# Row stores issued by SyncE and half of the cap computed by GpSimd in the message pass of a graph network kernel

## The reference, cut to what matters

```python
total = concat([atom_fea[dst], atom_fea[src], edge_fea], axis=1)
total = batchnorm(total @ fc_w.T + fc_b, bn1_w, bn1_b)
gate, core = split(total, 2, axis=1)
messages = sigmoid(gate) * softplus(core)
aggr = segment_sum(messages, dst)
```

## Time and profile before

| | |
|---|---|
| Median of three runs | 10762.31 us (10761.59 to 10765.0) |
| The profiled execution | 10770.62 us, of which the span in the trace is 10768.9 us |
| Message pass, first to last exp (L1103) | 5573.0 to 6329.5 us |
| VectorE, GpSimd, TensorE busy in the span | 62%, 65%, 52% |
| ScalarE busy in the span, and in 5700 to 6300 us | 21%, 81% |

### The profile page before, as it was taken

How to read it: one execution, slowest core, us unless ns; L and a number is a source line. 1 busy time by engine, 2 the same in 40 slices (tenths; PEclk the granted TensorE clock), 3 DMA queues, 4 the chain that set the end, 5 groups by cost and what they waited for, 6 DMA issues and landing times.

```text
span 10768.9 us, 124090 instructions
## 1 busy us (share of the span) xinstructions
PE 5555.5 (52%) x33901; PEld 4489.6 (42%) x33999; DVE 6624.7 (62%) x9196; ACT 2252.0 (21%) x3204; POOL 6998.2 (65%) x7048
## 2 busy tenths in 40 slices
PE   4566666457777566666654433333333433333333
PEld 3444444357777454545432213333333333333333
DVE  6777777888831455555568865555555555555556
ACT  1111111146620011111138841111111111111111
POOL 6777777523411777777765546777777577777774
PEclk8877777678989788888865555666556665555556
DMA  8777777423466677777756634555555345555552
GB/s 180 197 196 194 200 193 197 121 114 153 165 242 270 209 231 240 233 239 234 238 196 203 201 112 104 123 126 124 126 124 125 82 119 124 125 124 126 124 126 69
DMA packets 2332510, 1784.10 MB, mean 166 GB/s; under 512 B 1805237, under 2 KB 1977018, under 8 KB 2322746
## 3 DMA queue, kind: packets, MB, share of 16 engines
q1 hardware_dynamic: 759943, 879.12, 24.9%
q10 hardware_dynamic: 1356944, 617.91, 21.0%
q0 software_dynamic: 215456, 284.72, 11.5%
HBM read 921.34 MB, written 861.11 MB: 166 GB/s over the span
## 4 chain that ended last, share of the span: by engine, by line
POOL 54%; issue 22%; DVE 8%; DMA 6%; PE 4%; ACT 4%; SPq 1%; ACTq 1%; POOLq 0%; DVEq 0%
POOL arena L592 51%; DMA arena<-near_d,dlo 2%; ACT arena L1103 2%; DMA feat<-adj_d 2%; PE ph L914 2%; POOL feat L684 2%; DVE obuf L1881 1%; POOL sum_d L625 1%; ACT obuf L1073 1%; DMA arena<-in_x_dram,idx_src 1%; ACTq L1076 1%; DVE neg L1881 1%; ACT arena L1105 1%; ACT arena L1109 1%; PE pn L898 0%
## 5 line engine op out<-in xcount | busy, mean ns | idle before, releaser
L592 POOL DMA_INDIRECT arena<-table_d,idx_src x3136 | 2960.2, 944 | 1122.1 <-issue 955.0
L756 PE MATMUL pn<-work,wblk 128*128 128x128 f32 x3136 | 1049.5, 438 | 2387.7 <-DMA arena<-table_d,idx_src 2387.7
L756 PEld LDWEIGHTS pn<-work,wblk 128*128 128x128 f32 x3136 | 837.8, 327 | 2526.7 <-issue 1841.6
L592 POOL DMA_INDIRECT arena<-in_x_dram,idx_src x1568 | 1494.8, 953 | 514.7 <-issue 470.7
L592 POOL DMA_INDIRECT arena<-tsrc_d,idx_src x1568 | 1480.4, 944 | 477.7 <-issue 477.7
L1365 DVE TENSOR_SCALAR idx_src<-src_all 128x8 int32 (+1 forms) x784 | 142.8, 183 | 2320.7 <-PE pn L757 1590.6
L757 PE MATMUL pn<-ident,arena 128*128 128x128 f32 x4704 | 1373.5, 391 | 0.0
L757 PEld LDWEIGHTS pn<-ident,arena 128*128 128x128 f32 x4704 | 1174.8, 306 | 0.0
L1463 DVE STREAM_TRANSPOSE arena<-work 128x512 f32<-128x512 f32 x1568 | 990.8, 679 | 98.4 <-DVE work L1424 98.4
L1424 DVE TENSOR_TENSOR_SCAN work<-keep,work,pn 128x512 f32<-128x512 bf16 x588 | 752.5, 1280 | 247.1 <-PE ph L769 202.5
L746 PE MATMUL pn<-work,weT 128*128 128x512 f32 x784 | 549.3, 790 | 667.9 <-DMA arena<-tsrc_d,idx_src 638.8
(11 more groups left out here) (402 smaller groups left out, 11149.6 us busy)
## 6 DMA issues: line engine op xcount, KB each, us to landing
runs_d<-arena ACTq DMA_DIRECT2D x2352, 192.0 KB
adj_d<-feat SPq DMA_DIRECT2D x37, 3136.0 KB, 10.7
feat<-adj_d SPq DMA_DIRECT2D x37, 3136.0 KB, 11.0
seed_d<-nothing SPq DMA_DIRECT2D x392, 256.0 KB
arena<-seed_d SPq DMA_DIRECT2D x392, 256.0 KB, 7.0
attr<-in_edge_attr_dram SPq DMA_DIRECT2D x392, 256.0 KB
feat<-total_d SPq DMA_DIRECT2D x196, 512.0 KB
keep<-keep_d SPq DMA_DIRECT2D x588, 128.0 KB
```

Of the source, the lines that this page charges most:

```text
L592: g.indirect_dma_start(out=to, out_offset=None, in_=table, in_offset=bass.IndirectOffsetOnAxis(ap=idx, axis=0))\
L756: mm(to, wblk[:, PNA.index(p), j, :], feat_to[u], start=True, stop=False, skip_group_check=True)
```

## The change

ScalarE's `rows_out` keeps the copy but no longer waits for it and no longer issues the store. SyncE issues the stores, with a new function `rows_store(i, u)` that waits for the copy of that step. In SyncE's loop of the message pass the store of the step four before, `rows_store(i - 1, u)`, is put behind the loads and the mask of each u; the last four stores follow the loop. GpSimd scales the core's half first, then the gate's half, waits for its own first result, and takes the minimum of the core's half and 80; VectorE takes the minimum for the gate's half alone. `s_arg`, which ScalarE's exp waits for, now counts two for each step, one from each engine.

```diff
-        s_arg = ring("s_arg", one((SOFT, MSG)))
+        s_arg = ring("s_arg", {SOFT: 1, MSG: 2})
+            def rows_store(i, u):
+
+                s_rev.done(sp, MSG, i, u)
+                sp.dma_start(runs1_d.rearrange("(h n) c -> h n c", h=2)[:, bass.ds(blk(i, u) * BLK, BLK), :]
+                             .rearrange("h (p j) c -> p h (j c)", j=J),
+                             obuf_f[:, u * BLK:(u + 1) * BLK].rearrange("p (h q) -> p h q", h=2)).then_inc(s_out.sems[u], 16)
...
                                     attr_load(p, i, u)
                                     attr_load(p, i, u + 1)
                                     mask_load(p, i, u)
+                                rows_store(i - 1, u)
                             elif p == SOFT:
...
+                if p == MSG:
+                    for u in range(U):
+                        rows_store(IT - 1, u)
...
-                for part in range(2):
+                for part in (1, 0):
                     g.tensor_scalar(zbuf[:, u, part * BLK:(part + 1) * BLK], totals[:, u, part * BLK:(part + 1) * BLK],
                                     bnsc[:, part:part + 1], bnbi[:, part:part + 1], ALU.mult, ALU.add).then_inc(s_col.sems[u], 1)
+                s_col.part_done(g, MSG, i, u, 1)
+                g.sem_inc(s_in_order, 1)
+                g.tensor_scalar(ebuf[:, u, BLK:], zbuf[:, u, BLK:], CAP, None, ALU.min).then_inc(s_arg.sems[u], 1)
...
                     .then_inc(s_rev.sems[u], 1)
-                s_rev.done(act, MSG, i, u)
-                act.dma_start(runs1_d.rearrange("(h n) c -> h n c", h=2)[:, bass.ds(blk(i, u) * BLK, BLK), :]
-                              .rearrange("h (p j) c -> p h (j c)", j=J),
-                              to.rearrange("p (h q) -> p h q", h=2)).then_inc(s_out.sems[u], 16)
...
                 s_col.done(dve, MSG, i, u)
-                TS(ebuf[:, u, :], zbuf[:, u, :], CAP, None, ALU.min).then_inc(s_arg.sems[u], 1)
+                TS(ebuf[:, u, 0:BLK], zbuf[:, u, 0:BLK], CAP, None, ALU.min).then_inc(s_arg.sems[u], 1)
```

## The result

The changed kernel takes 11055.35 us (median of 4 runs, 11046.89 to 11061.92), the kernel before 10763.65 us beside it: a ratio of 1.027, with an interval of 1.0252 to 1.0288. It is 292 us slower; 10974 us was forecast, with a range of 10880 to 11080.

The account below looks back on a forecast made before the run. Two rings of about 3.8 us were taken to set the message-pass step; afterwards 2.62 + 0.90 + 3.9 + 2.6 = 10.0 us per pair against 7.76, so 212 us more: 10762 + 212 = 10974 us, range 10880 to 11080.

Parts of the forecast that it names:

- the forecast case: Message pass at about middle values, 10.0 us per two steps: 10974 us, own range 10900 to 11035, chance 0.62.
- the heavier ring: Rival: stores cost their whole 0.74 us, GpSimd at its mean, 11.5 us a pair, 11111 us; one or both, chance 0.19.
- GpSimd's minimum well over 1.1 us: Sign of being wrong: GpSimd's third operation, priced like a scaling (763 ns least, 1087 mean), takes much longer.
- The step that decides: SyncE's next loads wait for the end of copy k, not scan k: 5.7 us later against 2.5 us of slack.
- the ring: Message-pass loop ScalarE's copy, SyncE's store and load, GpSimd, exp: 10.0 us for two steps against 7.76.
- exp to the copy's end: First term, on ScalarE: exp of step k+3 starts, log, copy of step k ends; 2.62 us.
- copy's end to the load's issue: Second term, on SyncE: sees the copy, issues the store, then the load; 0.73 to 1.07 us, taken as 0.90.
- load to GpSimd's start: Third term: load of step k+5 issued until GpSimd starts on it; 3.80 and 3.96 us, taken as 3.9.
- the rival that charged 0.74 us for it: Stores ahead of loads on SyncE's queue add 0.74 us, load term 4.65; this, GpSimd's mean, or both: chance 0.19.
- GpSimd's start to exp: Fourth term: GpSimd's three operations of step k+5 until its exp starts; 2.3 to 3.3 us, taken as 2.6.
- The rival in which GpSimd's load made VectorE the limit: A draw: VectorE's operations at their longest beside busier GpSimd, 3.9 us, loads hidden; 10762 us, chance 0.04 with another route.
- VectorE's ring: Log, softplus, cap, exp in the message pass: said to fall from 3.80 to about 3.56 us a step.

Follow-up runs that it names:

- two_op_min: Changed kernel with GpSimd's minimum written as multiply by 1.0, then min 80, in one instruction: 11137.64 us.
- cap_only: Changed kernel with the stores given back to ScalarE, GpSimd keeping the minimum of the core's half: 10797.67 us, ratio 1.0031 to the kernel before.
- late_full: Changed kernel with each store two steps later in SyncE's order and the whole cap back on VectorE: 10727.88 us, ratio 0.995 to the kernel before.
- late_stores: Changed kernel, both parts kept, with each store two steps later in SyncE's order: 10768.92 us, ratio 1.0008 to the kernel before.
- column_min: Changed kernel with GpSimd's minimum taken against a column of 80s in SBUF instead of the constant: 11071.05 us.
- one_step_later: Changed kernel, both parts kept, with each store one step later in SyncE's order: 10790.63 us, ratio 1.002 to the kernel before.
- stores_only: Changed kernel with GpSimd's minimum given back to VectorE, SyncE still issuing the stores: 10960.56 us, ratio 1.0182 to the kernel before.
- early_cap: late_full with VectorE's cap put ahead of its softplus: 10724.42 us, ratio 0.9948 to the kernel before.
- scale_for_min: Changed kernel with GpSimd's minimum replaced by multiply and add with columns of 1 and 0, that half uncapped: 10995.42 us.
- longer_pool_program: Kernel before with 24 one-column memsets added to GpSimd's program ahead of the message pass: 10791.74 us.

## Why the prediction was right

**How near.** 11055 us lies in the stated range, 81 us above the forecast and 20 us above the forecast case's own range (10900 to 11035): it falls between that case and the heavier ring. One of the prediction's own signs of being wrong came, "GpSimd's minimum well over 1.1 us". That the range still held it is in part luck: the minimum's excess was softened by GpSimd's two scalings, which were quicker than taken, and nothing in the sum stood for the 26 us outside the pass.

**The step that decides held.** The loads were said to be paced by the end of copy k instead of scan k; SyncE's waits show it, moving the stores two steps on undoes it with nothing else changed, and one step is nearly enough. The sign, the place and the mechanism were those forecast.

**The terms of the ring.** Forecast 2.62 + 0.90 + 3.9 + 2.6 = 10.0 us a pair. Over the seven pairs from the exp at 5906.10 to that at 5980.10 us the changed kernel took 74.00 / 7 = 10.57 us:

- exp to the copy's end, 2.63 us: as forecast.
- copy's end to the load's issue, 0.79 and 1.35 us by turns, 1.03 on average over the seven: 0.13 more than the 0.90 taken, and every second one above the upper bound of 1.07.
- load to GpSimd's start, 3.6 to 4.5 us, 3.9 on average: as forecast. The Trainium skill (DMA: Bandwidth & Descriptors, section Issuing engines are not separate DMA queues) says that transfers issued by different engines share the same DMA engines all the same, so that moving an issue saves only the issuer's time; by that rule this term stays, and the trace agrees. A store of 256 KB directly ahead on the same queue added nothing to what the 3.9 us of the kernel before may already hold, and the rival that charged 0.74 us for it was wrong.
- GpSimd's start to exp, 3.00 us (5913.76 to 5916.76): 0.4 more than the 2.6 taken. This is the mis-sized term. I priced a minimum like a scaling, between 0.76 and 1.09 us; it took 1.48, and the two scalings 1.52 together.

Summed, 2.63 + 1.03 + 3.9 + 3.00 = 10.56 us against 10.57 measured and 10.02 forecast; 95 x 0.55 = 52 us, of which GpSimd's term has 38. With 212 this makes 264, and the pass grew by 263. The other 26 us of the profiled execution (2.6 ahead of the pass, 23 in the gathers after it) were not in the forecast at all.

**The half cap.** Forecast 0.44 us; 0.42 in two_op_min, 0.69 and 0.82 by turns in the changed kernel, beside the minimum. In the ring it did not matter, since the exp that belongs to it waits for GpSimd. Most of the gain that halving should have brought is taken by this stretching, though: in cap_only its mean was 583 ns, against 691 for the whole cap.

**The port.** The Trainium skill (SBUF — State Buffer, section Who interferes with whom) says that, of a VectorE operation in a two-port mode and one of GpSimd, whichever issues first has the shared ports for its whole instruction and the other blocks. The trace agrees only in part; in which mode the half cap ran, no run shows. Above, it starts at 5915.31, just behind GpSimd's minimum (5915.25 to 5916.73), takes 0.82 us and is done 0.60 us before it: it lost 0.40 us, not the whole instruction. Beside GpSimd's longer operation in two_op_min it lost nothing:

```profile
5902.85 2.00 POOL L616 TENSOR_SCALAR arena<-arena 128x512 f32<-128x512 f32 x1
...
5903.97 0.42 DVE L1445 TENSOR_SCALAR arena<-arena 128x512 f32<-128x512 f32 x1
```

The stretching is real; what sets its size is open. GpSimd's scalings and VectorE's two-input operations in the changed kernel, 5700 to 6500 us, against the earlier trace rows:

```profile
L612 POOL TENSOR_SCALAR arena<-feat,bnsc,bnbi 128x512 f32<-128x512 f32 x304 | 270.3, 899 | 311.9 <-DMA feat<-total_d 311.9
...
L1450 DVE TENSOR_TENSOR work<-arena 128x512 f32<-128x512 f32 x152 | 123.8, 814 | 76.7 <-ACT arena L1115 72.0
...
L1554 DVE TENSOR_TENSOR work<-work,arena 128x512 f32<-128x512 f32 x152 | 105.3, 693 | 18.3 <-DVE work L1434 8.0
```

GpSimd's scalings and both of VectorE's two-input operations got shorter on average; I put this down to the ring, in which they mostly run while the other engine waits, but no run tests it. The rival in which GpSimd's load made VectorE the limit had nothing to bite on.

**What the profile was to show.** ScalarE idles before every other exp, released by GpSimd, by 3.6 us where 2 to 3.5 were forecast. The DMA share fell from 61% to 43% (61 x 7.76 / 10.57 = 45). The hole between copy and gate closed. The exps come in twos of 3.76 and 6.90 us rather than 3.2 and 6.8: the short step is VectorE's ring, where I had named ScalarE's. And SyncE waits for a copy twice a pair (152 times in 800 us), not once; only the second holds up loads.

## What to carry to other kernels

Moving a cheap issue to an idle engine moves its wait too: ask what stands behind it in that engine's order, which event releases it now, and whether that event comes after the work which those followers feed. If it does, a ring is closed, and its length over its number of steps is the new time per step, however idle the engine looks. The remedy tried here is distance in that order: one step later took away the loss in the pass, and with two, and the whole cap on VectorE, late_full came out 0.5% faster than the kernel before.

## What the runs showed of the hardware that was not expected

A minimum on GpSimd over 128x512 f32 takes 1477 ns at the least, 1549 against a column, 1930 with a multiplication before it; multiply and add by columns, in one instruction over the same tensors, take 762 at the least.

After a message pass in which GpSimd takes minima, the indirect loads of the last two passes are 7 or 8 ns slower each, at 3,136 of them some 23 us. GpSimd's gathers in the changed kernel, those of the last two passes and those of the pass before the messages:

```profile
L603 POOL DMA_INDIRECT arena<-table_d,idx_src x3136 | 2983.0, 951 | 1121.8 <-issue 955.1 <-DMA table_d<-tab 166.6
...
L603 POOL DMA_INDIRECT arena<-tsrc_d,idx_src x1568 | 1479.6, 944 | 478.0 <-issue 478.0
```

In each of the changed kernel, cap_only, late_stores, two_op_min, column_min and one_step_later the first mean is 7 or 8 ns above the second (951 over 944 in four of them, 954 over 946 in column_min and one_step_later). In the kernel before, stores_only, late_full, early_cap, scale_for_min and longer_pool_program, which take no minimum on GpSimd, the two are within 1 ns, at 944 or at 946. Both levels occur on one and the same chip, so the two passes are compared within one execution. Neither a third operation nor a longer program does it; why a minimum should is open, and was not tried further.
